# VectorE's transposition of a finished unit, moved from the front of a step to behind the next unit's residual addition

## The reference, cut to what matters

```python
def reference(x, ...):
    x = x + conv_ref(layernorm_over_channels(x))  # fft2 then ifft2 (the identity), GroupNorm with 8 groups,
                                                   # w1 (64x64), relu, w2 (64x64), plus the block's own input
    t = tokens(x)                                  # (8, 16384, 64)
    t = t + ffn_ref(layernorm(t))                  # gate logits of 32 experts, softmax over the 16384 tokens,
                                                   # 8 best tokens of each expert, pooled row -> 65x256 -> gelu
                                                   # -> 257x64, added back to those 8 tokens
    return images(t)
```

## Time and profile before

| | us |
|---|---|
| median of 3 runs | 618.75 (618.2 to 620.87) |
| the profiled execution | 622.79 |
| its span, from the first to the last instruction | 620.6 |
| TensorE busy (matmul) | 480.7 (77%) |
| VectorE busy | 470.8 (76%) |
| ScalarE busy | 417.7 (67%) |
| GpSimd busy | 272.6 (44%) |
| mean granted TensorE clock, 1.0 being full speed | 0.881 |

### The profile page before, as it was taken

One profiled execution on the slowest core, in us unless ns is written; L12 is line 12 of the kernel. 1 busy time (PEld: TensorE's weight loads), 2 busy tenths in 40 slices (PEclk: granted clock), 3 DMA queues, 4 the chain that ended last, 5 costly groups with the idle time before them and its releaser, 6 DMA issues. The chain is left out here.

```text
span 620.6 us, 12857 instructions
## 1 busy us (share of the span) xinstructions
PE 480.7 (77%) x4964; PEld 198.6 (32%) x4964; DVE 470.8 (76%) x833; ACT 417.7 (67%) x635; POOL 272.6 (44%) x340
## 2 busy tenths in 40 slices
PE   5558799989988997898899889867886764688600
PEld 1222243333333333332333333322332222476500
DVE  6657576798699879978998998799797997964200
ACT  3556599888879987999799888966653565432000
POOL 1038161344009334714760484256864752220774
PEclk9859899999889999999999999998887979556755
DMA  7994367866656864776577666522233443000000
GB/s 271 371 419 141 125 202 231 307 208 205 207 206 208 251 224 163 240 218 262 176 243 259 208 203 205 193 115 102 76 110 120 124 144 103 6 5 1 13 13 8
DMA packets 36475, 106.85 MB, mean 172 GB/s; under 512 B 5176, under 2 KB 6200, under 8 KB 32320
## 3 DMA queue, kind: packets, MB, share of 16 engines
q1 hardware_dynamic: 34368, 105.00, 50.1%
q0 software_dynamic: 2048, 1.05, 0.9%
HBM read 71.95 MB, written 34.08 MB: 171 GB/s over the span
## 5 line engine op out<-in xcount | busy, mean ns | idle before, releaser
L1537 POOL TENSOR_TENSOR xs<-xs,us 128x1024 f32<-128x1024 f32 x64 | 150.9, 2377 | 113.6 <-DVE gsum L1009 51.0
L1017 DVE SCALAR_TENSOR_TENSOR xs<-cv,vecs,xs 128x1024 f32<-128x1024 f32 x64 | 81.9, 1280 | 23.3 <-PE cv L442 22.8
L442 PE MATMUL cv<-hid,w2bd 64*64 64x512 f32 x512 | 73.3, 645 | 20.4 <-ACT hid L796 20.0
L796 ACT ACTIVATE hid<-cv,b1n 128x1024 f32<-128x1024 f32 x64 | 70.9, 1107 | 19.2 <-PE cv L434 19.1
L1024 DVE STREAM_TRANSPOSE tok<-xs 128x1024 f32<-128x1024 f32 x64 | 79.4, 1240 | 0.6
L434 PE MATMUL cv<-us,w1n 64*64 64x512 f32 x512 | 70.8, 623 | 9.7 <-DVE xs L1017 9.7
L1009 DVE CUSTOM_DVE_ANT_0 us<-us,bc 128x1024 f32<-128x1024 f32 x60 | 72.5, 1209 | 6.4 <-PE bc L546 5.2
L470 PE MATMUL tl<-xs,gcen 128*32 128x256 f32 x1024 | 77.1, 424 | 0.4 <-ACT us L803 0.4
L845 ACT ACTIVATE junk<-us 128x1024 bf16<-128x1024 f32 x64 | 67.5, 1055 | 8.2 <-DVE gsum L1009 6.3
L546 PE MATMUL bc<-rstd_s,spread 32*128 32x256 f32 x368 | 49.2, 346 | 30.2 <-DVE rstd_s L1087 10.1
L826 ACT ACTIVATE sqx<-xs 128x1024 f32<-128x1024 f32 x64 | 66.4, 1049 | 1.7 <-PE st L423 1.7
(11 more groups left out here) (244 smaller groups left out, 670.6 us busy)
## 6 DMA issues: line engine op xcount, KB each, us to landing
us<-in_raw SPq DMA_DIRECT2D x64, 512.0 KB, 5.3
xs<-in_x SPq DMA_DIRECT2D x32, 1024.0 KB, 4.9
out_rows<-tok SPq DMA_DIRECT2D x64, 512.0 KB, 4.6
us<-in_e_w SPq DMA_DIRECT2D x8, 260.0 KB
xs<-in_e_w SPq DMA_DIRECT2D x8, 256.0 KB
sqc<-out_rows,idx_all POOLq DMA_INDIRECT x32, 2.4
out_rows<-sqc,idx_all POOLq DMA_INDIRECT x32, 2.1
vecs<-in_b SPq DMA_DIRECT2D x4, 0.2 KB, 6.5
```

The source lines that it names most:

```text
L442: mm = pe.matmul(cv[C * h:C * h + C, CH * sl:CH * sl + CH], w2bd[r, r], hid[r, CH * h:CH * h + CH], start=True, stop=True)
L796: nc.scalar.activation(hid[:], cv[:], ACT.Relu, bias=b1n[:, par:par + 1]).then_inc(h_done, 1)
L1017: nc.vector.scalar_tensor_tensor(out=xu, in0=cv[:], scalar=vecs[:, 3:4], in1=xu, op0=ALU.add, op1=ALU.add).then_inc(x1_done, 1)
L1537: nc.gpsimd.tensor_tensor(xu, xu, su, ALU.add).then_inc(s_done, 1)
```

## The change

`turn` of the unit before keeps its instruction, its waits and its signal. It leaves the head of VectorE's step and now stands behind `x1` and `norm_bias`, in front of `ln2_variance` and of the uses of jobs (s, 1) and (s, 2). Nothing else is touched, and no other engine's order changes.

```diff
                 mid = p1 and t >= 0
-                if b >= 0:
-                    turn(b, u)
                 if s == NU - 1 and p1:
                     norm_reduce(n)
...
                 x1(it, par, s)
                 if s == NU - 1 and p1:
                     norm_bias(n)
+                if b >= 0:
+                    turn(b, u)
                 if s == 0 and t >= 0:
                     ln2_variance(t)
...
                 use_at(it, (s, 1))
```

## The result

The changed kernel takes 627.79 us (median of 4 runs, 625.71 to 630.66), the kernel before 618.48 on the same chip (4 runs, 617.34 to 620.87): ratio 1.0118, 95% interval 1.008 to 1.0157, or 4.9 to 9.7 us slower. The forecast was 625.9, slower. (Ratios and intervals are those on record with each comparison; they are not the quotient of the two medians, which here is 1.0151.)

A forecast was written before the change was run, and what follows sets the result against it. No single engine bounds it: the ring x1, conv1, relu, conv2, x1 does, with extra work queued in each engine's order. Terms summed to +7.2 us on the 618.75 median, giving 625.9 us, range 615.5 to 633.

The forecast's parts named there:

- steps 2 to 3, images 1 to 6: TensorE's spread product (3, 0) waits for the later use, delaying centre, conv2 and x1 by 1.10 us each: +6.6.
- steps 0 to 1, images 2 to 6: The turn fills the variance's wait for ScalarE's square, so x1 comes 1.05 or 1.17 us earlier: -5.5.
- steps 0 to 1, images 1 and 7: Without that wait the turn pushes back the variance and ScalarE's logarithm, 0.6 us each: +1.2.
- image 1, steps 1 to 2: No logits are searched in steps 0 and 1, so this step is short of cover too: +0.5 us.
- steps 4 to 5: The late use delays the spread product and x1: +0.2 us in images 2 to 4, +0.5 in image 0, total +1.1.
- steps 6 to 7: The last unit's sum is read later, so ScalarE's squares and line 1039 move 0.25 us back, seven images: +1.8.
- image 0, steps 1 to 3: Late copies delay TensorE's product and conv1 by 1.06 us and ScalarE's squares by 0.4: together +1.5.
- faster rival: If conv2 of step 3 has cover, late uses cost nothing and step 0's gain remains: 613.3 us, 13 in 100.
- SyncE's queue: The store waits for the turn with the next raw load behind it, 1.17 us late; costed at nothing.
- Steps 5 to 6: TensorE has two groups of sums in front of conv1, so the late use costs nothing; 0.5 without that cover.
- clock rival: Added TensorE standstill brings one more low-clock stretch in each of six images, 8.9 us more: 634.8, 12 in 100.

The follow-up runs named there:

- later stores: Changed kernel with SyncE's order edited so each store, and the x load of step 0, goes one step later: 627.56 us, then 626.78 when timed again.
- third profile: The changed kernel with nothing edited, timed once more beside the changed kernel with each store one step later: 629.27 us, ratio 1.0172.

## Why the prediction was right

The mechanism was right, and so was the way the sum comes out. Below are the prediction's terms beside the x1-to-x1 times of the two traces. Ten intervals that differ by 0.6 to 1.7 us, and in which only one profile has a low stretch or has more of one, are left out. Without them the loop is 6.1 us longer.

| term | predicted | measured |
|---|---|---|
| steps 2 to 3, images 1 to 6 | +6.6 | +6.2 (1.12 to 1.14 in five, 0.55 in image 6) |
| steps 0 to 1, images 2 to 6 | -5.5 | -5.0 |
| steps 0 to 1, images 1 and 7 | +1.2 | +2.0 (1.45 and 0.56, the second with a low stretch in both profiles) |
| image 1, steps 1 to 2 | +0.5 | +0.4 |
| steps 4 to 5 | +1.1 | +0.7 (0.59 in image 0, 0.03 in images 2 to 4) |
| steps 6 to 7 | +1.8 | +1.0 in five images (0.13 to 0.30 each) |
| image 0, steps 1 to 3 | +1.5 | +1.1 in steps 1 to 2; 2 to 3 can't be compared |
| sum | +7.2 | +6.4 |

- **Steps 2 to 3.** 1.10 forecast, 1.13 measured in five images, with line 1005 named as what the product waits for. Image 6, taken as one of six alike, lost only half of it. The faster rival, which let conv1 decide and not the use, fell with that row, and the kernel with the turn moved in step 2 alone showed that this one place carries the loss.
- **Steps 0 to 1, images 2 to 6.** The wait is filled as worked out. With SyncE out of the way the step is 6.65, the 1.05 forecast from 7.70 to the hundredth; in image 3, where 1.17 was forecast, it falls by 1.34, from 7.99 to the same 6.65.
- **SyncE's queue: the step that failed.** I costed it at nothing because a raw load would be late by 1.17 where the step grows by as much. I looked at the shortest step, and the growth of 1.1 there did cover it. The steps 0 to 1 get shorter, and there nothing covered it. I also took a load to land in 5.3 us as before and looked only at the store. In steps 0 and 1 the late store holds an x load as well, and both now go out just in front of the raw load: it is mostly queued 0.6 to 0.7 us late, and behind the 1024 KB of the x load it lands in 7.2 to 8.2 us in step 0, where it took 3.9 to 5.7. In steps 0 to 1 that costs 1.1 to 1.5 us: image 1 lost 1.45, and 0.61 with the stores out of the way, which is the forecast of 0.6. With the turns later still it cost 10 us.
- **Small terms.** In image 0 steps 1 to 2 lost 1.10, where 1.06 was forecast. In steps 2 to 3 the mean granted clock is 0.81 before and 0.90 after, so their 0.6 us less say nothing of the 0.4 forecast for them. Image 7's 0.56 may be the clock's: in the first profile with later stores, nearly without a low stretch in that step, it takes 6.63 as before. Steps 5 to 6, forecast at nothing, cost 0.12 to 0.14 in images 2 to 4.
- **The clock rival.** The changed kernel's three profiles have four, five and six low stretches in images 1 to 6, the kernel before eight, so on balance there are not more of them. But the rival's mechanism occurs. In the third profile two of the six begin directly behind the added standstill, in images 3 and 5; centre and conv2 behind it take 1.93 and 1.95 us instead of 1.09 and 1.04, and steps 2 to 3 take 7.80 and 7.77. Image 3 of that profile:

```profile
245.82 0.50 PE L546 MATMUL bc<-rstd_s,spread 32*128 32x256 f32 x4 [1.26 <-DVE lg L1005]
246.25 1.93 PE L450 MATMUL tl<-us,cen 64*64 64x512 f32 x8
247.94 1.95 PE L442 MATMUL cv<-hid,w2bd 64*64 64x512 f32 x8
```

The Trainium skill (TensorE: Matmul & The Clock Gate, section What's actually happening) says that activity releases the throttle; these two cases agree with it, and 15 other standstills of 1.26 us in the three profiles were not followed by a low stretch.

- **The rest.** The three comparisons give 8.5 to 9.9 us between medians, the steps 6.1 to 6.4, and executions at one clock 6.5 to 8.3. The steps' sum lies within the intervals of the first two comparisons (4.9 to 9.7 and 3.5 to 10.9 us) and below that of the third (7.3 to 14). In the third, 3.3 us in the profile are the two low stretches just named; what else lies between, some 2 to 4 us by the medians and up to 2 at one clock, is not attributed. Since the sum of the steps came out under the forecast of 7.2 and the whole time above it, part of the nearness of 625.9 to 627.79 is luck.

## What to carry to other kernels

Where every engine runs a fixed order, as here, moving an instruction past others changed the sums of busy time by less than 0.4 us per image; what it cost lay in who waits for those others: for each one that becomes later, ask which engine has it in front of its ring. A wait that nothing else uses is a good place for filler, but the filler's own consumers, here a store in an in-order queue with loads behind it, move too. Such a chain is best moved at both ends: the turn behind the uses without the later store gave 625.7 us, the later store without any later turn 641.0, both 615.4.

## What the runs showed of the hardware

- How soon a raw load of 512 KB lands goes here with how close in front of it an x load of 1024 KB went out. In step 0 of images 1 to 5 it took 7.2 to 8.2 us with the x load 0.5 us in front (changed kernel) and 3.9 to 5.7 with it 2.3 us in front (before). A store of 512 KB made little difference: in steps 2 and 3, without an x load, the raw load took 4.2 to 5.2 us with a store 0.5 us in front, and 3.8 to 4.7 with one 0.4 us behind (later stores). The store does gain by its place: 3.2 us (median of 22) with a raw load behind it, 5.2 (median of 19) behind a raw load.
- The stretches at 1.2 instead of 2.4 GHz lie at different places in profiles of one kernel. What one costs depends on where it lies: nothing in step 1 of image 2 before the change (8.47 us, as in images 3 to 6 without one), 0.5 to 1.0 us in step 1 with later stores, 1.6 to 1.7 in steps 2 to 3 of the changed kernel's third profile.
- Eight profiles have the turn right behind x1 in step 1, and in each of images 1 to 6 TensorE stands still there for a use: 48 cases. In 27 of them for 1.17 us; behind nine of these a low stretch begins within a microsecond, and in one during it. In the other 21, of 0.32 to 1.07 us, none begins. What decides among the 27 is not shown.
